# A gated attention block with eight experts on one core: new queue orders and cheaper gated sums in the last stage

## The chip, the cores and the metric

The kernel runs on one core of a Trainium2 chip. The core has TensorE (PE: matrix products, with weight loads PEld beside them), VectorE (DVE), ScalarE (ACT), GpSimd (POOL) and SyncE (SP, which here only issues DMAs). Each engine takes its own queue in order and meets the others only at semaphores. The metric is the device time of one execution in microseconds (us); lower is better.

## The reference

There are 32 sequences of 128 positions and 128 channels, all float32. Each is normalised, attends to a context (16 heads of 8 channels), and the gated result is added to x; then comes this block, whose output is again gated and added:

```python
x1 = _layer_norm(x + attn_out, ln1_w, ln1_b)           # x: normalised input of the block
gates = softmax(x1 @ gate_w.T + gate_b)                # 8 experts
top_gates, top_idx = top_k(gates, 2)
expert_outputs = einsum('bsd,efd->bsef', x1, expert_w) + expert_b
moe_out = sum(expert_outputs[top_idx] * top_gates)
out = x + tanh(g_ffn) * _layer_norm(x1 + moe_out, ln2_w, ln2_b)
```

## The kernel before

The first part, both attentions (`pe_attention`, `dve_attention` and so on), takes some two thirds of the span and isn't touched except for its constants. It leaves every sequence's attention result in `att_all` and the block's input in `xn2_all`.

The last stage (`z_pe`, `z_act`, `z_dve`, `z_pool`, `z_sp`) works on 16 groups g of two sequences (G = 2, W = 256 columns, NE = 8 experts, HALF = 4). It is a software pipeline written out by hand: every engine runs steps s = -1 to 20, and in step s its queue holds work of several groups, s to s - 4, in a fixed order; semaphores give the data order. For one group the work goes like this:

- ScalarE copies the attention result (`fetch`, z_att), TensorE transposes it (`transpose_att`), ScalarE copies that (`copy_att`, z_att_t), TensorE multiplies by the output weights (`project`).
- VectorE adds the input (`attention_sum`, z_h) and makes mean and variance; GpSimd makes the factor of the norm (`factor1`: z_ve, then a power, z_rstd); VectorE normalises (`normalise1`, z_n); GpSimd applies weight and bias (`x1`: z_nw, z_x).
- TensorE transposes z_n (`transpose_n`), ScalarE copies it with weight and bias (`copy_x1`, z_x_t). TensorE makes the logits (`logits`), then experts 0 to 3 (`experts`, k = 0, one product of 512 columns for each sequence) and, a step later, experts 4 to 7 (k = 1).
- Gates: VectorE adds the bias and takes the maximum (`shift_logits`), ScalarE takes the exponentials (`gates_exp`), VectorE finds the two best of eight and scales (`gating`: MAX8, z_sum, z_two, z_rsum, MATCH_REPLACE8, z_top, z_gates). z_two is a copy of the two largest values into a tile whose other six places hold -1.
- Experts 0 to 3 are gated and summed on VectorE in eight instructions (`experts` in `z_dve`, z_acc, on top of z_x). Experts 4 to 7 are gated on ScalarE in eight instructions (`gate_experts`, z_gated) and summed by TensorE through products with the identity (`gated_sum`), together with the experts' bias times the transposed gates (`gates_t`, `copy_gates`). For each sequence that is one product with the bias and four with the identity, 128 columns each.
- VectorE adds both halves (`all_experts`, z_x_moe) and makes the second norm's mean and variance, GpSimd its factor (`factor2`, z_rstd_), VectorE normalises (`normalise2`, z_y), GpSimd applies weight, bias and the residual (`final`: z_yw, z_ywb, z_o), SP stores (z_out).

The order on each queue in a step, with the group that each belongs to, is the `body` of each function. On VectorE it is:

```python
shift_logits(s - 2); normalise1(s - 1); normalise2(s - 4)
gating(s - 2); experts(s - 2); attention_sum(s); all_experts(s - 3)
```

Float32 products are recorded as two MATMUL entries each, so "x8" of a group is four products.

## Time and profile before

| | |
|---|---|
| median of three runs | 482.83 us (482.69 to 483.07) |
| the profiled execution | 483.01 us |
| its span, first to last instruction | 480.8 us |
| mean granted TensorE clock | 0.975 |
| busy share TensorE, VectorE, ScalarE, GpSimd | 87%, 80%, 57%, 65% |

The profile is of one execution. A row of a timeline gives the start on the span's clock, the time from the start of the first to the end of the last instruction that is merged into it (xN), and in brackets how long the engine stood idle before it and what released it. "f32<-f32" shapes are partitions x elements in each partition. A granted clock of 1.00 is 2.4 GHz for TensorE, 0.50 is 1.2 GHz. Instructions of one engine overlap by some tens of ns, so durations add up to a little more than the queue's time; where that matters, starts are compared.

### The profile page before, as it was taken

To read this page: it belongs to the slowest core of one execution; us is meant where nothing else is said; L and a number is where in the kernel's file an instruction comes from. 1 tells how busy PE (TensorE), PEld (TensorE's weight loads), DVE (VectorE), ACT (ScalarE), POOL (GpSimd) and SP (SyncE) were. 2 spreads that over 40 slices of the span, in tenths; PEclk is the share of its full clock that TensorE was granted. 3 is DMA by queue.
4 is the path that set the end of the run, shared out by engine and by line. 5 is a ranking of instruction groups with operands and counts; after the bars stand their busy time and mean duration, and the time that the engine had idled before them with its cause. 6 is when DMAs were issued, how large, how long until landed. Compare 5 with 4: busy or idle time off the path is not lost.

```text
span 480.8 us, 18054 instructions
## 1 busy us (share of the span) xinstructions
PE 420.6 (87%) x6804; PEld 265.6 (55%) x6804; DVE 382.6 (80%) x1205; ACT 273.5 (57%) x693; POOL 313.5 (65%) x688
## 2 busy tenths in 40 slices
PE   0378888888888999999999999997899999999983
PEld 0245454544445566666666666664467676767652
DVE  5688999999978878788877787832679899999971
ACT  1136777777676666675666666673354545454440
POOL 5465766767798888878887874220346666666654
PEclk9999999999999999999999999997699999999995
DMA  7855776755533444333344334200000000000000
GB/s 165 195 151 161 194 187 166 184 148 130 134 93 106 110 118 113 95 96 103 104 122 114 94 96 115 66 10 1 1 1 24 11 25 11 24 11 25 12 23 22
DMA packets 88022, 42.78 MB, mean 89 GB/s; under 512 B 15992, under 2 KB 87808, under 8 KB 87936
## 3 DMA queue, kind: packets, MB, share of 16 engines
q1 hardware_dynamic: 77072, 38.87, 30.6%
q10 hardware_dynamic: 10864, 2.76, 2.6%
q8 instruction: 55, 0.90, 0.8%
q14 instruction: 31, 0.25, 0.2%
HBM read 5.68 MB, written 2.10 MB: 16 GB/s over the span
## 4 chain that ended last, share of the span: by engine, by line
PE 37%; DVE 18%; POOL 3%; ACT 2%; issue 2%; ACTq 0%; POOLq 0%; DVEq 0%
PE u_bank L443 8%; DVE z_acc L969 5%; PE s_bank L381 5%; PE s_bank L394 4%; PE s_bank L799 2%; PE u_bank L820 2%; DVE r L617 2%; PE st_bank L799 2%; PE t_bank L373 2%; POOL z_rstd_ L697 2%; PE t_bank L367 2%; PE u_bank L456 2%; PE st_bank L394 2%; DVE z_two L945 1%; DVE z_y L994 1%
## 5 line engine op out<-in xcount | busy, mean ns | idle before, releaser
L636 DVE TENSOR_REDUCE nm<-s_bank 128x4 f32<-128x512 f32 x256 | 171.5, 682 | 37.6 <-PE s_bank L394 34.6
L526 ACT ACTIVATE pt<-st_bank 128x512 f32<-128x512 f32 x256 | 149.1, 601 | 77.2 <-PE u_bank L443 41.1
L394 PE MATMUL s_bank<-qk 64*64 64x128 bf16 (+1 forms) x1536 | 102.5, 221 | 12.2 <-DVE nm L636 7.7
L443 PE MATMUL u_bank<-pt,vaug 128*32 128x128 f32 x2048 | 109.5, 286 | 1.6 <-DVE ao L653 0.3
L394 PE MATMUL st_bank<-qk 64*64 64x128 bf16 (+1 forms) x1588 | 101.7, 218 | 0.0
L394 PEld LDWEIGHTS s_bank<-qk 64*64 64x64 bf16 (+1 forms) x1536 | 72.9, 104 | 36.1 <-issue 18.8
L394 PEld LDWEIGHTS st_bank<-qk 64*64 64x64 bf16 (+1 forms) x1588 | 72.1, 103 | 0.0
L443 PEld LDWEIGHTS u_bank<-pt,vaug 128*32 128x32 f32 x2048 | 40.8, 108 | 27.2 <-issue 3.8
L381 PE MATMUL s_bank<-mqk,idb 64*64 64x256 bf16 x256 | 38.3, 291 | 2.7 <-ACT pt L526 0.8
L884 ACT ACTIVATE z_gated<-s_bank,z_gates 128x128 f32<-128x128 f32 x64 | 18.3, 369 | 35.7 <-PE u_bank L820 35.7
L381 PE MATMUL st_bank<-mkq,idb 64*64 64x256 bf16 x256 | 38.3, 293 | 0.1
L290 POOL TENSOR_TENSOR part<-r,part 128x512 bf16<-128x512 f32 x32 | 37.1, 1159 | 1.4
L820 PE MATMUL u_bank<-z_gated,idf 128*128 128x128 f32 x256 | 38.0, 293 | 0.0
L799 PE MATMUL s_bank<-ewt,z_x_t 128*128 128x512 f32 x64 | 36.1, 647 | 0.5 <-DVE z_acc L969 0.5
L301 POOL TENSOR_SCALAR mst<-nm 128x16 bf16<-128x16 f32 x64 | 13.2, 207 | 34.3 <-DVE nm L636 34.3
L820 PEld LDWEIGHTS u_bank<-z_gated,idf 128*128 128x128 f32 x256 | 31.8, 195 | 4.0 <-issue 0.2
L799 PE MATMUL st_bank<-ewt,z_x_t 128*128 128x512 f32 x64 | 33.6, 607 | 0.0
L456 PE MATMUL u_bank<-idf,us 128*128 128x128 f32 x128 | 28.0, 300 | 5.4 <-ACT us L542 5.4
L533 ACT ACTIVATE mts<-m_bank 128x128 bf16<-128x128 bf16 x64 | 17.8, 278 | 24.5 <-PE m_bank L451 24.5
L695 POOL TENSOR_SCALAR z_ve<-z_mv 128x2 f32<-128x2 f32 x16 | 3.1, 193 | 43.7 <-DVE z_mv L913 43.6
L381 PEld LDWEIGHTS s_bank<-mqk,idb 64*64 64x64 bf16 x256 | 14.5, 103 | 26.8 <-issue 18.4
L285 POOL TENSOR_SCALAR part<-r 128x512 bf16<-128x512 f32 x32 | 19.9, 620 | 13.4 <-DVE r L617 7.1
(121 smaller groups left out, 883.0 us busy)
## 6 DMA issues: line engine op xcount, KB each, us to landing
qk<-part SPq DMA_DIRECT2D x221, 128.0 KB, 2.8
x_all<-x SPq DMA_DIRECT2D x16, 128.0 KB, 2.8
qk<-qrow SPq DMA_DIRECT2D x32, 64.0 KB, 2.2
qk<-mts ACTq DMA_DIRECT2D x64, 32.0 KB, 2.5
out<-z_o SPq DMA_DIRECT2D x16, 128.0 KB, 1.8
c_all<-ctx_in SPq DMA_DIRECT2D x14, 128.0 KB, 3.2
ewt<-exp_t SPq DMA_DIRECT2D x1, 512.0 KB
qk<-part ACTq DMA_DIRECT2D x3, 128.0 KB, 2.7
```

The source lines that it names most:

```text
L285: pool.tensor_scalar(part[u % 2][:, 1:2 * PARTS:PARTS, :], r32[:, :].rearrange("c (o t) -> c o t", o=2), 1.0, 0.0, ALU.mult, ALU.add).then ...
L290: pool.tensor_tensor(part[u % 2][:, 2:2 * PARTS:PARTS, :], r32[:, :].rearrange("c (o t) -> c o t", o=2), part[u % 2][:, 1:2 * PARTS:PARTS, ...
L381: pe.matmul(to, idb[rows, rows], mask[rows, rows].unsqueeze(1).broadcast_to([64, HEADS, 64]), start=True, stop=False, skip_group_check=True)
L394: ins = pe.matmul(to[outs, :], fixed[:, outs], moving, start=not masked, stop=True, skip_group_check=masked)
L443: ins = pe.matmul(u_bank[b][32 * j:32 * j + 32, r * P:(r + 1) * P], v, pt[m % 4][:, j, :], start=half == 0, stop=half == 1, skip_group_che ...
L456: ins = pe.transpose(u_bank[q % 2][:, W + r * P:W + (r + 1) * P], us[q % 2][:, r * P:(r + 1) * P], idf[:, :])
L526: act.activation(pt[m % 4][:, :, :].rearrange("k j q -> k (j q)"), st_bank[m % 2][:, :], ACT.Exp).then_inc(ex, 1)
L636: dve.tensor_reduce(nm[q % 2][:, first:first + HEADS], s_bank[n % 2][:, :].rearrange("q (j k) -> q j k", j=HEADS), AX_X, ALU.max, negate=T ...
L799: ins = pe.matmul(e_bank[b][k][:, :], zx1t[i][:, b * P:(b + 1) * P], ewt[:, k * 512:(k + 1) * 512], start=True, stop=True)
L820: ins = pe.matmul(dst, idf[:, :], zyg[:, b, e, :], start=False, stop=e == HALF - 1)
L884: ins = act.activation(zyg[:, b, e, :], e_bank[b][1][:, e * P:(e + 1) * P], ACT.Copy, scale=zg[i][:, b, HALF + e:HALF + e + 1])
L969: dve.scalar_tensor_tensor(out=zacc[i][e % 2][:, b, :], in0=e_bank[b][0][:, e * P:(e + 1) * P], scalar=zg[i][:, b, e:e + 1], in1=zacc[i][( ...
```

## The change

1. VectorE: `normalise2` leaves its queue. The copy z_two goes: the six smaller places of z_sorted are filled with -1 in place. `gated_pairs` is new: it adds z_gated of experts 4, 5 to those of 6, 7 for both sequences in one instruction of 512 elements in each partition (z_gated_pairs). `gating` and `gated_pairs` move ahead of `normalise1`.
2. ScalarE: `fetch` goes (TensorE transposes straight from `att_all`), `normalise2` comes as two activations (z * factor + offset), and `copy_gates` moves ahead of `copy_x1`.
3. TensorE: the gated sum takes both sequences at once: one product of 256 columns with the bias (the gates of both sequences transposed together to 16 rows, the bias laid out twice on the diagonal in `ebs`), and two of 256 columns with the identity. The order in a step becomes experts 1, transpose_att, gated_sum, gates_t, transpose_n, project, logits, experts 0.
4. GpSimd: `factor2` also makes the offset -mean * factor (one element for each sequence). `x1` now comes first in a step, `final` after it and a step later; the store is a step later too.
5. Constants: one more DMA (25 instead of 24) brings the second copy of the bias; `ebs` (16 x 256) is set to zero at the start, and SP waits for that.

```diff
-                elif 9 <= s <= 10:
-                    later_constants(sp, 3 * s - 9, 3 * s - 6)
+                elif 9 <= s <= 10:
+                    later_constants(sp, 4 * s - 18, min(4 * s - 14, LATER))
...
+                pe.transpose(u_bank[1][0:G * NE, W:W + P], zg[i][:, :, :].rearrange("q b e -> q (b e)"), idf[:, :]).then_inc(z_gt, 1)
+
+            def gated_sum(g, gc):
+                i = gc % 2
+                pe.wait_ge(z_gtc, g + 1)
+                pe.wait_ge(z_yp, g + 1)
                 if gc >= 1:
                     pe.wait_ge(z_all, (g - 1) * ALL + 1)
-                for b in range(G):
-                    ins = pe.transpose(u_bank[0][0:NE, W + b * P:W + (b + 1) * P], zg[i][:, b, :], idf[:, :])
-                ins.then_inc(z_gt, 1)
-
-            def gated_sum(g, gc):
-                i = gc % 2
-                pe.wait_ge(z_gtc, g + 1)
-                pe.wait_ge(z_yg, g + 1)
-                for b in range(G):
-                    dst = u_bank[0][:, b * P:(b + 1) * P]
-                    pe.matmul(dst, zgt[i][:, b * P:(b + 1) * P], ebs[:, :], start=True, stop=False)
-                    for e in range(HALF):
-                        ins = pe.matmul(dst, idf[:, :], zyg[:, b, e, :], start=False, stop=e == HALF - 1)
+                dst = u_bank[0][:, 0:W]
+                pe.matmul(dst, zgt[i][:, :], ebs[:, :], start=True, stop=False)
+                for e in range(HALF // 2):
+                    ins = pe.matmul(dst.rearrange("q (b d) -> q b d", b=G), idf[:, :], zyp[:, :, e, :],
+                                    start=False, stop=e == HALF // 2 - 1)
                 ins.then_inc(z_yb, 1)

             def body(s, c):
-                if in_z(c, 0):
-                    transpose_att(s, c)
                 if in_z(c, 2):
                     experts(s - 2, c - 2, 1)
                 if in_z(c, 0):
-                    project(s, c)
+                    transpose_att(s, c)
+                if in_z(c, 3):
+                    gated_sum(s - 3, c - 3)
+                if in_z(c, 2):
+                    gates_t(s - 2, c - 2)
                 if in_z(c, 1):
                     transpose_n(s - 1, c - 1)
-                if in_z(c, 3):
-                    gated_sum(s - 3, c - 3)
+                if in_z(c, 0):
+                    project(s, c)
                 if in_z(c, 1):
                     logits(s - 1, c - 1)
                     experts(s - 1, c - 1, 0)
-                if in_z(c, 2):
-                    gates_t(s - 2, c - 2)
...
+            def normalise2(g, gc):
+                act.wait_ge(z_rs2, (g + 1) * 4)
+                if gc >= 2:
+                    act.wait_ge(z_fin, (g - 2) * FIN + 1)
+                for b in range(G):
+                    act.activation(zy[gc % 2][:, b, :], zsum[:, b, :], ACT.Identity, bias=znb2[:, b:b + 1],
+                                   scale=zrs2[:, b:b + 1]).then_inc(z_y2s, 1)
...
+                if in_z(c, 4):
+                    normalise2(s - 4, c - 4)
+                if in_z(c, 2):
+                    copy_gates(s - 2, c - 2)
                 if in_z(c, 1):
                     copy_x1(s - 1, c - 1)
-                if in_z(c, -1):
-                    fetch(s + 1, c + 1)
                 if in_z(c, 2):
                     gate_experts(s - 2, c - 2)
-                    copy_gates(s - 2, c - 2)
...
-                dve.tensor_copy(ztwo[:, :, 0:2], z8[:, :, 0:2]).then_inc(z_gate, 1)
+                dve.memset(z8[:, :, 2:NE], -1.0).then_inc(z_gate, 1)
...
+            def gated_pairs(g, gc):
+                dve.wait_ge(z_yg, g + 1)
+                if gc >= 1:
+                    dve.wait_ge(z_yb, g)
+                dve.tensor_tensor(zyp[:, :, :, :], zyg[:, :, 0:HALF // 2, :], zyg[:, :, HALF // 2:HALF, :],
+                                  ALU.add).then_inc(z_yp, 1)
...
-                    dve.tensor_scalar(zy[:, b, :], zsum[:, b, :], zmv2[:, b, 0:1], zrs2[:, b:b + 1],
-                                      ALU.subtract, ALU.mult).then_inc(z_y2s, 1)
...
                 if in_z(c, 2):
                     shift_logits(s - 2, c - 2)
+                if in_z(c, 3):
+                    gated_pairs(s - 3, c - 3)
+                if in_z(c, 2):
+                    gating(s - 2, c - 2)
                 if in_z(c, 1):
                     normalise1(s - 1, c - 1)
-                if in_z(c, 4):
-                    normalise2(s - 4, c - 4)
                 if in_z(c, 2):
-                    gating(s - 2, c - 2)
                     experts(s - 2, c - 2)
...
+                rstd_of(pool, zmv2[:, :, 1], zve2[:, :], zrs2[:, :], z_rs2, g * 4)
+                pool.wait_ge(z_rs2, g * 4 + 2)
+                for b in range(G):
+                    pool.tensor_scalar(znb2[:, b:b + 1], zmv2[:, b, 0:1], zrs2[:, b:b + 1], -1.0,
+                                       ALU.mult, ALU.mult).then_inc(z_rs2, 1)
...
-                if in_z(c, 4):
-                    final(s - 4, c - 4)
                 if in_z(c, 1):
                     x1(s - 1, c - 1)
+                if in_z(c, 5):
+                    final(s - 5, c - 5)
...
+            sp.wait_ge(c_two, 1)
...
-            dve.memset(ztwo[:, :, :], -1.0).then_inc(c_two, 1)
+            dve.memset(ebs[:, :], 0.0).then_inc(c_two, 1)
```

## Rows read from the trace of the kernel before

**Rows 1.** Stretches: busy us (instructions) of each engine, granted clock, DMA share, GB/s.

```profile
20.00:40.00 20.00, 15.17 (x164) 8.79 (x164) 15.60 (x33) 6.96 (x16) 10.02 (x27) 1.00 0.59 159
331.00:334.00 3.00, 2.31 (x8) 1.53 (x8) 0.30 (x1) 0.76 (x3) 0.00 (x0) 0.50 0.00 0
414.20:422.30 8.10, 8.10 (x44) 5.53 (x43) 7.42 (x36) 4.17 (x16) 5.44 (x9) 1.00 0.07 19
```

**Rows 2.** Timeline, VectorE, one step: start us, us, engine, line, instruction.

```profile
414.21 0.60 DVE L994 TENSOR_SCALAR z_y<-z_x_moe,z_mv_,z_rstd_ 128x128 f32<-128x128 f32 x2 [0.33 <-POOL z_rstd_ L697]
414.73 0.23 DVE L942 MAX8 z_sorted<-z_exps 128x8 f32<-128x8 f32 x2
...
415.00 0.65 DVE L945 COPY z_two<-z_sorted 128x4 f32<-128x4 f32 x1
...
416.75 0.35 DVE L969 SCALAR_TENSOR_TENSOR z_acc<-s_bank,z_gates,z_x 128x128 f32<-128x128 f32 x1
...
421.07 0.14 DVE L930 TENSOR_TENSOR z_logit<-u_bank,gbb 128x16 f32<-128x16 f32 x1
...
421.37 0.60 DVE L922 TENSOR_SCALAR z_n<-z_h,z_mv,z_rstd 128x128 f32<-128x128 f32 x2
422.29 0.60 DVE L994 TENSOR_SCALAR z_y<-z_x_moe,z_mv_,z_rstd_ 128x128 f32<-128x128 f32 x2 [0.33 <-POOL z_rstd_ L697]
```

**Rows 3.** All instructions of one tile, duration ns min/median/max: z_two, then z_top.

```profile
L945 DVE COPY z_two<-z_sorted x16: 169/648/651, 340.4 to 463.0; 128x4 f32<-128x4 f32 x16
...
L952 DVE TENSOR_TENSOR z_top<-z_exps,z_others x16: 175/376/381, 341.3 to 463.7; 128x16 f32<-128x16 f32 x16
```

**Rows 4.** Timeline of GpSimd over the same step.

```profile
414.90 0.73 POOL L1029 TENSOR_TENSOR z_yw<-z_y,l2w 128x256 f32<-128x256 f32 x1 [0.72 <-DVE z_y L994]
...
418.02 0.73 POOL L1022 TENSOR_TENSOR z_x<-z_nw,l1b 128x256 f32<-128x256 f32 x1
420.13 0.19 POOL L695 TENSOR_SCALAR z_ve<-z_mv 128x2 f32<-128x2 f32 x1 [1.39 <-DVE z_mv L913]
420.41 0.70 POOL L697 TENSOR_TENSOR z_rstd<-z_ve,mhalf 128x2 f32<-128x2 f32 x1
```

**Rows 5.** Timeline of VectorE at the kernel's start.

```profile
1.25 0.07 DVE L1123 MEMSET z_two<- 128x16 f32 x1
```

**Rows 6.** Timeline of VectorE at 8.7 us.

```profile
8.73 0.69 DVE L612 TENSOR_TENSOR r<-t_bank,part 128x512 f32<-128x512 f32 x1
```

**Rows 7.** Timeline of TensorE over the same step.

```profile
416.18 0.48 PE L818 MATMUL u_bank<-ebs,z_gates_t 8*128 8x128 f32 x2
...
419.09 0.51 PE L787 MATMUL u_bank<-gwt,z_x_t 128*128 128x8 f32 x4
...
420.39 1.02 PE L799 MATMUL st_bank<-ewt,z_x_t 128*128 128x512 f32 x2
421.25 0.38 PE L809 MATMUL u_bank<-idf,z_gates 128*8 128x128 f32 x2
```

**Rows 8.** Timeline of ScalarE: one step's exponentials, and the last gated experts.

```profile
421.95 0.47 ACT L866 ACTIVATE z_exps<-z_logit,z_max 128x8 f32<-128x8 f32 x2
...
466.72 1.14 ACT L884 ACTIVATE z_gated<-s_bank,z_gates 128x128 f32<-128x128 f32 x4 [4.05 <-PE u_bank L820]
```

**Rows 9.** Timeline of VectorE: the first z_acc of three steps.

```profile
351.82 0.35 DVE L969 SCALAR_TENSOR_TENSOR z_acc<-s_bank,z_gates,z_x 128x128 f32<-128x128 f32 x1
...
457.47 0.35 DVE L969 SCALAR_TENSOR_TENSOR z_acc<-s_bank,z_gates,z_x 128x128 f32<-128x128 f32 x1
...
464.40 0.35 DVE L969 SCALAR_TENSOR_TENSOR z_acc<-s_bank,z_gates,z_x 128x128 f32<-128x128 f32 x1
```

**Rows 10.** Timeline of TensorE at the stage's start.

```profile
331.21 0.66 PE L761 MATMUL t_bank<-idf,z_att 128*128 128x128 f32 x2 [1.21 <-ACT z_att L846]
```

**Rows 11.** Timeline of VectorE, then of GpSimd, in the last steps.

```profile
473.27 0.42 DVE L980 TENSOR_TENSOR z_x_moe<-u_bank,z_acc 128x256 f32<-128x256 f32 x1 [3.70 <-PE u_bank L820]
...
476.28 0.72 POOL L1029 TENSOR_TENSOR z_yw<-z_y,l2w 128x256 f32<-128x256 f32 x1 [0.71 <-DVE z_y L994]
```

More of the change, by code:

```diff
@@ L43 @@
 AHEAD = 4
-LATER = 24
+LATER = 25
 LATE_STEP = 12
@@ L700, in two @@
             return [sb(f"{name}{i}", shape) for i in range(2)]
-        zat = two("z_att", [P, G, P])
         zo_t = two("z_att_t", [P, W])
@@ L721, in gated_block_kernel @@
         z_gate = sem("z_gate_steps"); z_exp = sem("z_gate_exp"); z_gt = sem("z_gates_transposed")
-        z_gtc = sem("z_gates_t_copied"); z_y = [sem(f"z_experts{k}") for k in range(2)]; z_yg = sem("z_experts_gated"); z_yb = sem("z_expert_bias")
+        z_gtc = sem("z_gates_t_copied"); z_y = [sem(f"z_experts{k}") for k in range(2)]; z_yg = sem("z_experts_gated"); z_yp = sem("z_gated_pairs_summed"); z_yb = sem("z_expert_bias")
         z_acc = sem("z_accumulated"); z_all = sem("z_all_summed_steps"); z_rs2 = sem("z_rstd2_steps"); z_y2s = sem("z_normalised2")
@@ L731, in z_steps @@
         def z_steps(body):
-            for s in range(-1, GROUPS + 5):
+            for s in range(GROUPS + 6):
                 body(s, s)
@@ L760, in transpose_att @@
                 for b in range(G):
-                    ins = pe.transpose(t_bank[:, b * P:(b + 1) * P], zat[i][:, b, :], idf[:, :])
+                    ins = pe.transpose(t_bank[:, b * P:(b + 1) * P], one(att_all, g * G + b), idf[:, :])
                 ins.then_inc(z_ot, 1)
```

60 lines of the change are left out of this document (26 added, 34 removed).

## The prediction

> **What bounds the kernel now.** I read the profile in this order: the page, the stretches, then the timeline of each engine over one step of the last stage, then the stage's first and last steps. The edit touches only that stage, which runs from the last attention product at about 331 us to the end of the span at 480.8. The stretches show what kind of stage it is: over one step TensorE is busy 8.10 of 8.10 us and VectorE 7.42, ScalarE 4.17, GpSimd 5.44, at full granted clock [rows 1]. So two engines are full at once. TensorE has no gap in a step, and VectorE's queue sets its length, 8.08 us: the second normalisation of one step starts at 414.21 and of the next at 422.29 [rows 2]. The chain that ended last follows VectorE through these steps. A cut that serves only one of the two would stop at once at the other; this edit cuts both.
>
> **VectorE, step by step.** Four things leave its queue or get cheaper, one comes.
>
> - The two z_y instructions go to ScalarE. They hold the queue from 414.21 to 414.73, 0.52 us, and it stood 0.33 us for their factor before; from z_n at 421.37 to z_y at 422.29 are 0.92 us where two such instructions alone need 0.52 [rows 2]. Away: 0.52 + 0.40 = 0.92.
> - The copy z_two lasts 0.17 us at its shortest and 0.65 in the median of 16 [rows 3]. In the step shown it started at 415.00, GpSimd's z_yw ran from 414.90 to 415.63, and the copy ended at 415.65 [rows 2, 4]: it was let in as GpSimd's instruction ended. In its place comes a fill of 12 elements, for which the fill of 16 elements, 0.07, is the nearest row [rows 5]. Freed: between 0.40 (if its start still costs some 0.25) and 0.58; I take 0.46.
> - z_top lasts 0.38 in the median against 0.17 at its shortest [rows 3]; I read it as the same contact. In the new order GpSimd stands waiting for z_n, which VectorE makes only after the gates, so it is idle through the gating. Freed: 0.20 (0 if something else of GpSimd falls there).
> - The sum in pairs is one VectorE instruction of 512 elements a row with both inputs in SBUF. No such row exists. The nearest is the 512-element subtraction with one input in PSUM, 0.69 us [rows 6]; the last 0.08 overlaps the next instruction, as in the pair of z_y (0.60 long, 0.52 held). I take 0.61, with 0.55 and 0.75 as ends.
>
> That is 8.08 - 0.92 - 0.46 - 0.20 + 0.61 = 7.11 us a step if nothing waits.
>
> **The wait for GpSimd.** The sum in pairs has what slowed z_top, two inputs in SBUF, so it may have to wait for GpSimd too. Let T be the end of z_n. GpSimd's five big instructions take from 414.90 to 418.75, 3.85 us [rows 4]; in the new order they follow z_n at once, so z_ve starts near T + 3.9 and the power behind it, 0.28 later and 0.70 long [rows 4], runs from 4.2 to 4.9. VectorE starts z_acc at T - 0.08, reaches the logits 4.32 later (416.75 to 421.07) and is through with them 0.30 after that (421.37) [rows 2]: the sum in pairs is due at T + 4.54, inside the power. If the power holds it off as z_yw did the copy, it gets in about 0.1 before the recorded end, at 4.81: a wait of 0.27. Ends: 0 if so small an instruction as the power doesn't hold it off, and 0.73 if it always arrives with a GpSimd instruction just begun. I take 0.27: **7.38 us a step, 0.70 less.**
>
> On this the Trainium skill (SBUF — State Buffer, section "SBUF: two separate sides") has a rule: a VectorE instruction with two SBUF inputs, or in a two-port mode, and a GpSimd instruction exclude each other for a whole instruction, whoever starts first. The rows of z_two and z_top agree. By the rule the step is 7.38 or up to 7.84; without it 7.11.
>
> **Do the others keep up?** TensorE: the gated sum takes 2.91 us now (416.18 to 419.09: ten products of 128 columns) [rows 7]. A product of 512 columns takes 0.86 (420.39 to 421.25) [rows 7], so one of 256 about 0.43 and three 1.3, with 0.1 to change over: 1.4, ends 1.3 and 1.9 (six times the 0.29 that 128 columns cost now, and the same 0.1). One of two gate transposes goes, 0.1. TensorE needs 8.1 - 1.5 - 0.1 = 6.5 us. Its order is the other danger: the second half of the experts, the gated sum and the gate transposes now stand ahead of the transposes of z_n. It restarts after z_acc, T + 2.1; experts 0 and 1 are four products of 512 columns, 3.5, the transpose of the next attention about 0.2: T + 5.8. There the pairs are ready (4.81 + 0.69 = 5.5), the gated sum ends at 7.2, the gate transpose at 7.3, and z_n of the next step is there at 7.38. Were it late, it would catch up where it now waits for z_acc: its queue alone, with about 0.4 for the copy of z_n's transpose in which it has only the projection to do, needs 6.9.
>
> ScalarE gives up the copy of the attention and gets two rows of 128 elements. By its z_gated row (four in 1.14, some 0.25 apart) [rows 8] and for two per-row operands more, 0.25 to 0.45 each; it had 4.2 of 8 us, so this hides. GpSimd gets two factors of one element a row, some 0.2 each beside a z_ve of 0.19 [rows 4]: 5.9 us with its gaps become 6.4, plus 0.6 in which the sum in pairs holds it: 7.0 of 7.38, still hidden, but with little left. The exponentials, 0.47 us for the pair [rows 8], run under the sum in pairs; were that shorter, MAX8 would wait for them, so the cover is needed.
>
> **The whole.** Between the second group's gating and the fifteenth's lie 13 steps, z_acc at 351.82 to 457.47, 105.65 us [rows 9]; at 7.38 they are 95.9, 9.7 less. The last interval, to 464.40, is 6.93 [rows 9]; new it holds z_acc 2.08, the second norm's sums 1.11 (what is left of the 4.32 beside z_acc and the first norm's 1.13), logits 0.30, pairs 0.61 + 0.27 and gating 1.36 (MAX8 at 414.73 to z_acc at 416.75 is 2.02 [rows 2], less 0.66) = 5.73: 1.2 less. Steps: -10.9.
>
> Fill: the first transposes needn't wait for a ScalarE copy (1.21 us idle before them [rows 10]), worth 0.5. Against it, the second projection now stands behind the transposes of z_n and ahead of the logits, at half clock [rows 1]: 1.2 us, half in the shade of ScalarE's copy, so 0.6. Together +0.1, ends -0.5 and +1.0.
>
> Drain, from the last z_acc X (464.40) to the end, is 16.4. Before, ScalarE's gated experts started only at 466.72, X + 2.3, behind the previous gated sum, and the last sum was ready for VectorE at 473.27, X + 8.9; final began at 476.28, 4.5 before the end [rows 8, 11]. New, they wait only for the previous pairs and the gates' transpose: X + 0.8 to 2.9, pairs to 3.7, gated sum to 5.1 (6.5 at half clock, which I take), the sums and factor 2.3 and 0.4 for the new factors: X + 9.2. But final of group 14 (three instructions of 0.73 with 0.08 between [rows 4], 2.3) now stands on GpSimd behind that factor and ahead of final of group 15: X + 9.2 + 2.3 + 4.5 = X + 16.0, that is -0.4, and -1.8 at full clock. I take -0.5.
>
> Start: a fill of 16 rows x 256 instead of 0.07 us [rows 5] stands ahead of the rows that SP waits for, +0.2 at most, taken in full. The one more constant is a single issue of some 0.5 us in a unit that has no input loads left: nothing; uncovered, 0.5.
>
> Sum: -10.9 + 0.1 - 0.5 + 0.2 = -11.1. The profiled execution took 483.01 (span 480.8 and 2.2 around it), so **471.9 us**; the median of three runs is 0.2 lower than that execution, which I leave out as within the measurement.
>
> **Rivals.**
>
> 1. *The power holds nothing off*: 7.11 a step, but MAX8 then waits 0.05 for the exponentials, 7.16: 14 x 0.22 = 3.1 us below the forecast, **468.8 us**. For it: the power handles two elements a row for 0.70 us [rows 4], so it hardly touches the memory. Against: z_top, just as small, was held off. Chance 0.13.
> 2. *The port costs a whole instruction*: GpSimd, 7.0 us full, falls behind until its big instructions, not the power, meet the pairs or the gating; 7.84 a step (7.11 + 0.73), 0.24 less than before; 14 x 0.46 = 6.4 us above the forecast, **478.3 us**. For it: z_two lost 0.48 in this way in its median step [rows 3]. Chance 0.12.
> 3. *TensorE takes over*: its queue sets the step once the gated sum takes over 1.9 us (6.9 + 0.5), and at 2.6, that is 0.86 for each product as if it had 512 columns, the step is the 8.1 of now: **482 to 484 us**. For it: ten small products take 0.29 each now, though a quarter of 0.86 is 0.21 [rows 7], so something beside the columns costs. Against: at 0.29 for each half of a 256-column product the sum is still only 1.9. Chance 0.06, no change.
> 4. *Slower: the clock.* TensorE, no longer full, is granted 1.2 GHz in mid-stage, as in 331 to 334, where it was busy 2.31 of 3 us [rows 1]. The step then goes by TensorE, 2 x 6.5 = 13.0 us: 14 x 5.6 = 79 us above the forecast, **about 551 us**. It decides if the clock falls for more than a tenth of the stage. Against: 15.17 busy of 20 us kept 2.4 GHz in 20 to 40 us [rows 1], and here it is 6.5 of 7.4. Chance 0.04. By itself: the Trainium skill (TensorE: Matmul & The Clock Gate, Part 1) says that the clock follows how busy the engine has lately been.
>
> **How the numbers follow.** The forecast has 0.65, with 470 to 475 as its own range (step 7.25 to 7.6). Range: rival 1 and the lower half of rival 2 come in, 468 to 478; out stay rivals 3 and 4 and half of 2, 0.16. A difference under 0.2%, 1 us, is no change here. Faster 0.65 + 0.13 + 0.12 = 0.90, same 0.06, slower 0.04.
>
> **What would show it.** z_acc starts 7.4 us apart; z_top at 0.17 and the fill under 0.1; the sum in pairs recorded at 0.7 plus its wait, ending behind a power; three gated products of 0.43; TensorE standing some 0.7 us before the experts; two finals in a row at the end. The prediction is wrong if the pairs stretch beyond 1.1 us, if GpSimd never stands idle, or if the granted clock falls.

## The result: 467.8 us, 3.2% less than before

| | before | changed |
|---|---|---|
| median (lowest to highest) of 4 runs | 482.95 us (482.69 to 483.79) | 467.79 us (466.28 to 468.27) |
| ratio (95% interval) | | 0.9678 (0.9655 to 0.9701) |
| the profiled execution | 483.01 us, span 480.8 | 467.32 us, span 465.5 |

The kernel is faster by 15.2 us where 11 were forecast: the time lies 4.1 us below the forecast and 0.2 below the range. Line numbers differ by a few between the two kernels; the names of tiles are the same.

I read the changed profile as I had read the other. First the stretches: a part of the kernel that the edit doesn't touch, one step of the last stage, and two stretches of its start (busy us and instructions of PE, PEld, DVE, ACT and POOL, granted clock, DMA).

```profile
20.00:40.00 20.00, 15.12 (x162) 8.84 (x164) 15.58 (x33) 6.78 (x15) 9.91 (x27) 1.00 0.60 160
400.00:407.03 7.03, 6.82 (x29) 3.96 (x28) 6.72 (x35) 4.49 (x16) 6.05 (x12) 1.00 0.06 19
335.70:341.40 5.70, 5.66 (x14) 3.62 (x15) 3.03 (x20) 1.05 (x3) 2.59 (x5) 0.50 0.00 0
341.40:345.00 3.60, 3.15 (x14) 1.61 (x12) 2.16 (x8) 0.90 (x3) 1.21 (x2) 0.98 0.00 0
```

20 to 40 us is as before [rows 1], so the difference lies in the last stage. In a step VectorE is busy 6.72 of 7.03 us and TensorE 6.82. Next the starts of z_acc: second, fifteenth and last step.

```profile
349.55 0.35 DVE L971 SCALAR_TENSOR_TENSOR z_acc<-s_bank,z_gates,z_x 128x128 f32<-128x128 f32 x1
```

```profile
441.33 0.34 DVE L971 SCALAR_TENSOR_TENSOR z_acc<-s_bank,z_gates,z_x 128x128 f32<-128x128 f32 x1
...
447.45 0.35 DVE L971 SCALAR_TENSOR_TENSOR z_acc<-s_bank,z_gates,z_x 128x128 f32<-128x128 f32 x1
```

From 349.55 to 441.33 are 91.78 us for 13 steps, 7.06 each (one of 7.38, then 7.03), where 105.65 stood [rows 9]. The chain of work that ended last, through one step, says whose 7.03 it is.

```profile
by line: PE s_bank L800 27.8%; PE st_bank L800 17.2%; PE u_bank L818 17.1%; PE u_bank L788 12.2%; ACT z_x_t L853 11.5%; PE u_bank L816 6.2%; PE t_bank L778 4.7%; PE u_bank L807 2.2%; PE t_bank L760 2.2%; issue 1.3%
...
407.94 0.57 ACT z_x_t L853
```

It no longer touches VectorE: TensorE's queue closes on itself, with one copy of ScalarE (z_x_t) inside. TensorE over the same step:

```profile
401.52 0.61 PE L788 MATMUL u_bank<-gwt,z_x_t 128*128 128x8 f32 x4 [0.21 <-ACT z_x_t L853]
401.99 1.10 PE L800 MATMUL s_bank<-ewt,z_x_t 128*128 128x512 f32 x2
...
405.50 0.38 PE L760 MATMUL t_bank<-idf,c_all 128*128 128x128 f32 x2
405.82 0.69 PE L816 MATMUL u_bank<-ebs,z_gates_t 16*128 16x256 f32 x2
406.44 1.13 PE L818 MATMUL u_bank<-z_gated_pairs,idf 128*128 128x256 f32 x4
407.41 0.27 PE L807 MATMUL u_bank<-idf,z_gates 128*16 128x128 f32 x1
407.52 0.38 PE L778 MATMUL t_bank<-idf,z_n 128*128 128x128 f32 x2
407.74 0.61 PE L770 MATMUL m_bank<-wo,z_att_t 128*128 128x128 f32 x4
408.55 0.61 PE L788 MATMUL u_bank<-gwt,z_x_t 128*128 128x8 f32 x4 [0.21 <-ACT z_x_t L853]
```

From start to start: logits 0.47, eight halves of experts 3.51, transposes of the attention 0.32, bias product 0.62, sum of the pairs 0.97, gates 0.11, z_n 0.22, projection with ScalarE's copy 0.81; together 7.03. No gap but the 0.21 after the projection, which the copy makes. And VectorE:

```profile
401.35 0.42 DVE L908 TENSOR_TENSOR z_h<-m_bank,xn_all 128x256 f32<-128x256 f32 x1
...
403.60 0.14 DVE L932 TENSOR_TENSOR z_logit<-u_bank,gbb 128x16 f32<-128x16 f32 x1
...
403.87 0.69 DVE L980 TENSOR_TENSOR z_gated_pairs<-z_gated 128x512 f32<-128x512 f32 x1
404.51 0.24 DVE L944 MAX8 z_sorted<-z_exps 128x8 f32<-128x8 f32 x2
...
404.82 0.07 DVE L947 MEMSET z_sorted<- 128x12 f32 x1
...
405.32 0.18 DVE L954 TENSOR_TENSOR z_top<-z_exps,z_others 128x16 f32<-128x16 f32 x1
405.53 0.17 DVE L956 TENSOR_TENSOR z_gates<-z_top,z_rsum 128x16 f32<-128x16 f32 x1
405.64 0.60 DVE L924 TENSOR_SCALAR z_n<-z_h,z_mv,z_rstd 128x128 f32<-128x128 f32 x2
406.17 0.34 DVE L971 SCALAR_TENSOR_TENSOR z_acc<-s_bank,z_gates,z_x 128x128 f32<-128x128 f32 x1
```

Its work takes 4.31 from z_acc to the logits (without 0.15 in which z_h waits for the projection), 0.27 to the pairs, 0.64 from there to MAX8, 1.13 from MAX8 to z_n, 0.53 for z_n: 6.88 us. What MAX8 waits for is on ScalarE:

```profile
403.99 0.49 ACT L867 ACTIVATE z_exps<-z_logit,z_max 128x8 f32<-128x8 f32 x2 [0.45 <-DVE z_max L935]
```

The exponentials end at 404.48 and MAX8 starts at 404.51. In the last step, where they had ended 0.26 us earlier, MAX8 follows the start of the pair sum at 0.61 (445.55 to 446.16). So the pair sum fills a wait that is there in any case, and 0.03 of the 6.88 is the rest of that wait. Now GpSimd at the time of the pair sum, and every instance of the pair sum (duration ns min/median/max).

```profile
403.50 0.70 POOL L698 TENSOR_TENSOR z_rstd<-z_ve,mhalf 128x2 f32<-128x2 f32 x1
404.29 0.31 POOL L696 TENSOR_SCALAR z_ve_<-z_mv_ 128x2 f32<-128x2 f32 x1
```

```profile
L980 DVE TENSOR_TENSOR z_gated_pairs<-z_gated x16: 685/685/693, 347.3 to 451.8; 128x512 f32<-128x512 f32 x16
```

The pair sum starts at 403.87 with GpSimd's power in progress (403.50 to 404.20), as foretold, and isn't held at all. It is 685 to 693 ns in all 16: 13 of them meet a power that had begun 0.35 us or more before, the other three meet z_ve_. What gives way is GpSimd's next instruction, z_ve_, which starts under the sum: 0.31 us here, 304 ns in the median of 16, 192 at its shortest.

**Where the 15.3 us of span come from.** Start of the stage (end of the last attention tile) 330.62 to 330.82: +0.2; from there to the second z_acc 21.20 to 18.73: -2.5; the 13 steps: -13.9; the last interval 6.93 to 6.12: -0.8; from the last z_acc to the end 16.4 to 18.05: +1.65.

### The profile page after: what moved, and what is told of

It is laid out like the page before. It is cut to its first block, busy times and chain, and to the rows that moved or that the text cites. A ratio compares the mean times of both kernels' runs of the same rounds, so it can differ in the third digit from the quotient of the medians.

```text
span 465.5 us, 17610 instructions
## 1 busy us (share of the span) xinstructions
PE 399.0 (86%) x6564; PEld 240.7 (52%) x6564; DVE 372.6 (80%) x1189; ACT 280.1 (60%) x709; POOL 324.2 (70%) x720
## 4 chain that ended last, share of the span: by engine, by line
PE 51%; ACT 4%; DVE 3%; POOL 1%; issue 1%; POOLq 0%; ACTq 0%; DVEq 0%
PE u_bank L445 9%; PE s_bank L800 6%; PE st_bank L800 6%; PE s_bank L383 5%; PE u_bank L818 4%; PE s_bank L396 4%; DVE r L619 2%; PE u_bank L816 2%; PE u_bank L788 2%; ACT z_x_t L853 2%; PE t_bank L375 2%; PE t_bank L369 2%; PE u_bank L458 2%; PE st_bank L396 2%; ACT part L506 1%
## 5 line engine op out<-in xcount | busy, mean ns | idle before, releaser
L800 PE MATMUL s_bank<-ewt,z_x_t 128*128 128x512 f32 x64 | 35.0, 629 | 0.0
L544 ACT ACTIVATE us<-u_bank 128x256 f32<-128x256 f32 x64 | 24.9, 389 | 0.7 <-PE u_bank L445 0.7
L646 DVE RECIPROCAL rec<-u_bank 128x16 f32<-128x16 f32 x64 | 15.9, 249 | 11.2 <-PE u_bank L458 11.2
L245 POOL TENSOR_TENSOR rstd<-ve,mhalf 128x2 f32<-128x2 f32 x32 | 22.8, 713 | 2.7
L458 PEld LDWEIGHTS u_bank<-idf,us 128*128 128x128 f32 x128 | 12.8, 140 | 19.0 <-ACT us L544 18.6
```

What stands on the lines that cost most here:

```text
L245: pool.tensor_tensor(rstd[u % 2][:, :], ve[u % 2][:, :], mhalf[:, :], ALU.pow).then_inc(rstd_s, 1)
L458: ins = pe.transpose(u_bank[q % 2][:, W + r * P:W + (r + 1) * P], us[q % 2][:, r * P:(r + 1) * P], idf[:, :])
L544: act.activation(us[q % 2][:, :], u_bank[q % 2][:, 0:W], ACT.Copy).then_inc(ucopy, 1)
L800: ins = pe.matmul(e_bank[b][k][:, :], zx1t[i][:, b * P:(b + 1) * P], ewt[:, k * 512:(k + 1) * 512], start=True, stop=True)
```

## The experiments

All stand against the changed kernel, but those named "before", and ratios are to the kernel before (483.1 to 483.4 us in these comparisons). Theory A: TensorE's queue sets 7.03 us and the power holds nothing off. Rival B: VectorE sets it, with waits for GpSimd in it. "Step" is z_acc to z_acc.

**1. no_pairs.** The sums in pairs go; TensorE adds eight experts in four products instead of four pairs in two.

```diff
-                for e in range(HALF // 2):
-                    ... zyp[:, :, e, :], start=False, stop=e == HALF // 2 - 1)
+                for e in range(HALF):
+                    ... zyg[:, :, e, :], start=False, stop=e == HALF - 1)
-                if in_z(c, 3):
-                    gated_pairs(s - 3, c - 3)
```

> The changed kernel without the sum in pairs: TensorE sums the four gated experts itself, with four identity products of 256 columns instead of two. VectorE's queue loses 0.64 us a step, TensorE's gets two products of 0.485. Theory A, TensorE's queue sets the changed kernel's step of 7.03 us: the step becomes 8.0, about 14 x 0.97 = 13.6 us more than the changed kernel, 481 us. Rival B, VectorE's queue sets the step and TensorE only trails it, as the prediction had it: the step falls to 6.4 to 7.0, 459 to 468 us.

Measured: 479.07 us, ratio 0.9941 (0.9911 to 0.9972), step 7.90.

```profile
405.13 1.99 PE L818 MATMUL u_bank<-z_gated,idf 128*128 128x256 f32 x8
406.96 0.27 PE L807 MATMUL u_bank<-idf,z_gates 128*16 128x128 f32 x1
```

```profile
403.20 0.24 DVE L944 MAX8 z_sorted<-z_exps 128x8 f32<-128x8 f32 x2 [0.56 <-ACT z_exps L867]
```

```profile
400.04 0.42 DVE L908 TENSOR_TENSOR z_h<-m_bank,xn_all 128x256 f32<-128x256 f32 x1 [0.93 <-PE m_bank L770]
```

VectorE's queue gets no shorter: from z_max to MAX8 it is 0.73 us with the pair sum and without it, since MAX8 waits for the exponentials. Then VectorE stands 0.93 us before every z_h. The step follows TensorE's sum, 1.83 from start to start instead of 0.97. A holds, with 0.86 us more and not the expected 0.97; but as VectorE was not relieved, this run could not have shown rival B's shorter step.

**2. no_bias_product.** Leaves out the experts' bias term, one product on TensorE.

```diff
-                pe.matmul(dst, zgt[i][:, :], ebs[:, :], start=True, stop=False)
-                ... start=False, ...
+                ... start=e == 0, ...
```

> The changed kernel without the product with the experts' bias (the output lacks that term), so 0.62 us less for TensorE in a step and nothing else moved. Theory A: TensorE falls to 6.4 us, VectorE's 6.88 us take over, the step goes from 7.03 to 6.9 and 14 x 0.15 = 2.1 us are saved, with the last gated sum at half clock shorter by 1.1 as well: 464.6 us. Rival B: only the end is shorter, 466.7 us. Were VectorE's own need less than 6.88, down to TensorE's 6.4: 459 us.

Measured: 464.87 us, 0.9609 (0.9580 to 0.9637), step 6.87. 0.62 us taken from TensorE shorten the step by 0.16; then VectorE is full, without an idle stretch, and TensorE waits 0.2 for z_acc. So VectorE's own need is 6.88 us, and TensorE led it by 0.15.

**3. norm2_on_vector.** z_y goes back from ScalarE to VectorE, behind z_n.

```diff
+            def normalise2(g, gc):      # VectorE
+                ...
+                    dve.tensor_scalar(zy[gc % 2][:, b, :], zsum[:, b, :], zmv2[:, b, 0:1], zrs2[:, b:b + 1],
+                                      ALU.subtract, ALU.mult).then_inc(z_y2s, 1)
                     normalise1(s - 1, c - 1)
+                if in_z(c, 4):
+                    normalise2(s - 4, c - 4)
```

> The changed kernel with the second normalisation's two instructions back on VectorE, behind the first normalisation; GpSimd's factors for it are ready by then. VectorE needs 6.88 + 0.52 = 7.4 us a step. Theory A (the larger of the two queues sets the step): 7.4 to 7.5 instead of 7.03, 14 x 0.4 = 5.6 us more, 473.4 us. If TensorE had room to spare behind VectorE (rival B) the whole 0.52 would show: 475 us.

Measured: 478.74 us, 0.9906 (0.9891 to 0.9920), step 7.79. VectorE, then GpSimd:

```profile
411.21 1.00 DVE L979 TENSOR_SCALAR z_y<-z_x_moe,z_mv_,z_rstd_ 128x128 f32<-128x128 f32 x2
```

```profile
411.38 0.75 POOL L1027 TENSOR_TENSOR z_nw<-z_n,l1w 128x256 f32<-128x256 f32 x1 [0.62 <-DVE z_n L922]
```

6.88 + 0.52 would be 7.40. The pair takes 1.00 instead of 0.60, since z_nw of GpSimd starts under it: 6.88 + 0.93 = 7.81. The move to ScalarE was worth more than its two instructions.

**4. gating_behind_norm.** VectorE makes z_n before the gates, so that GpSimd's five large instructions run beside the gating.

```diff
-                    gating(s - 2, c - 2)
-                if in_z(c, 1):
                     normalise1(s - 1, c - 1)
+                if in_z(c, 2):
+                    gating(s - 2, c - 2)
```

> The changed kernel with the gates back behind the first normalisation on VectorE. Then GpSimd's two instructions on z_n run while VectorE makes z_top and z_gates, which have two inputs in SBUF. Theory A with the exclusion by large GpSimd instructions: z_top is 0.38 long again, z_acc again waits 0.15 for the gates with nothing in between, VectorE needs 7.2 to 7.3 us a step, 470 to 472 us. If GpSimd's instructions don't hold it off: z_top stays at 0.18, step 7.03 to 7.05, 468 us.

Measured: 473.89 us, 0.9807 (0.9793 to 0.9822), step 7.45. VectorE, then GpSimd:

```profile
410.64 0.64 DVE L954 TENSOR_TENSOR z_top<-z_exps,z_others 128x16 f32<-128x16 f32 x1
```

```profile
410.52 0.73 POOL L1019 TENSOR_TENSOR z_nw<-z_n,l1w 128x256 f32<-128x256 f32 x1
```

z_top is held until z_nw ends (0.64 us, 0.176 in the changed kernel, and more than the 0.38 expected), and the first z_acc starts 0.27 after z_gates instead of 0.11. MAX8 no longer waits: 6.88 - 0.03 + 0.46 + 0.16 = 7.47, VectorE's queue. The power, which here starts under the pair sum, takes 1.05 instead of 0.70. The order of the change, with no large instruction of GpSimd beside the gating, is worth 0.4 us a step.

**5. sum_covers_copy.** On TensorE the gated sum goes between the transposes of z_n and the projection, to fill the 0.4 us of ScalarE's copy.

```diff
-                if in_z(c, 3):
-                    gated_sum(s - 3, c - 3)
                 if in_z(c, 2):
                     gates_t(s - 2, c - 2)
                 if in_z(c, 1):
                     transpose_n(s - 1, c - 1)
+                if in_z(c, 3):
+                    gated_sum(s - 3, c - 3)
```

> The changed kernel with one move on TensorE: the gates' transpose and the transposes of z_n go ahead of the gated sum, so that ScalarE's copy of the transposed z_n runs beside the gated sum and not beside the projection alone (TensorE's 0.36 us gap before the logits). Theory A: TensorE needs 6.7 us, VectorE's 6.9 take over, 14 x 0.13 = 1.8 us less than the changed kernel, 466.0 us. Rival B (VectorE sets the step already): 467.8, no change. A third way: the gated sum, 0.3 us later, makes the second sum on VectorE wait, 468 or more.

Measured: 474.30 us, 0.9819 (0.9804 to 0.9834), step 7.56. A miss. VectorE:

```profile
406.01 0.42 DVE L908 TENSOR_TENSOR z_h<-m_bank,xn_all 128x256 f32<-128x256 f32 x1 [0.59 <-PE m_bank L770]
```

TensorE's own gap is gone, but the projection is 1.6 us later, z_h waits 0.59 for it, and then TensorE waits for the gates and for z_n (0.37 and 0.24). The loop now runs through both engines and is longer than either queue.

**6. last_final_early.** On GpSimd the last step but one finishes before the last step's factors.

```diff
-                if in_z(c, 5):
+                if in_z(c, 5) and s - 5 != GROUPS - 2:
                     final(s - 5, c - 5)
+                if s - 4 == GROUPS - 2:
+                    final(s - 4, c - 4)
```

> The changed kernel with the last steps of GpSimd reordered: the final part of group 14 stands ahead of the last group's factor, not behind it. Theory: in the changed kernel two final parts stand one after the other at the end, the first of them, 2.3 us, on the path; here it fits into GpSimd's idle 2.0 us before the last factor, which it may delay by 0.3: 2.0 us less, 465.8 us. If the end isn't set by GpSimd's queue: 467.8.

Measured: 466.16 us, 0.9649 (0.9635 to 0.9664); 17.2 us from the last z_acc to the end, against 18.05.

```profile
452.86 0.67 PE L816 MATMUL u_bank<-ebs,z_gates_t 16*128 16x256 f32 x2 [3.12 <-DVE z_gated_pairs L980]
453.46 1.22 PE L818 MATMUL u_bank<-z_gated_pairs,idf 128*128 128x256 f32 x4
```

Here the last sum ran at full clock (1.82 us from start to end, 3.2 in the changed kernel), which explains 1.4 us, more than the 0.85 gained, so nothing is left for the order: the earlier finish ends at 457.70, delays the last factor (z_ve_ at 457.79, its input ready at 455.94), and the last z_yw then waits 0.99 us for ScalarE.

**7. filler_products.** Products into a bank that nobody reads, six while the stage starts and seven before the last gated sum, to keep TensorE at work.

```diff
+                if s == 1:
+                    filler(u_bank[0], 6)
+                if s == GROUPS + 2:
+                    filler(t_bank, 7)
```

> The changed kernel with products whose result nobody reads in two places where TensorE stands: six of 256 columns after the second group's first transposes (it stands 2.96 us there) and seven before the last gated sum (3.13 us). Theory: the granted clock falls to 1.2 GHz because TensorE stands, and 5.7 us of the start and the last gated sum (3.27 us) run at half speed; kept busy, the start saves 1.5 to 2.5 us and the end 1.5: 464 to 465 us. If the clock falls all the same: 467.8, or 0.5 more if the filler delays the work behind it.

Measured: 465.01 us, 0.9621 (0.9607 to 0.9636). Stretches of its start:

```profile
334.50:336.00 1.50, 1.50 (x5) 1.12 (x5) 0.31 (x3) 0.00 (x0) 0.91 (x2) 0.50 0.00 0
336.00:338.00 2.00, 2.00 (x11) 1.66 (x10) 0.43 (x2) 0.00 (x0) 1.42 (x2) 0.80 0.03 8
```

The clock falls all the same, but comes back at about 337 instead of 341.4; the fillers themselves hold up the transposes of z_n by 1.2 us. Stage start to second z_acc is 17.39 us (18.73), the last sum runs at full clock, the end takes 16.6. That the fillers keep the clock up at the end isn't shown, since the last sum begins at full clock in experiments 2 and 6 too, which have none.

**8. combined** (5, 6 and 7 together).

> The three moves together: gated sum beside ScalarE's copy, last final part early, filler products in both gaps. By the single expectations 1.8 + 2.0 + 3.5 = 7.3 us less than the changed kernel, 460.5 us; if only the first final part and the filler count, 462.3.

Measured: 472.37 us, 0.9767 (0.9751 to 0.9783), step 7.56: the order of 5 spoils the steps; 1.9 us better than 5 by itself, less than the 4.4 that 6 and 7 gained singly; both of them had the last sum at full clock already, and the clock falls at 330.9 here and comes back at 337.8, so that half clock lasts 6.8 us and not 3.4 as in 7.

**9. project_then_sum.** The gated sum goes behind the projection.

```diff
                 if in_z(c, 0):
                     project(s, c)
+                if in_z(c, 3):
+                    gated_sum(s - 3, c - 3)
                 if in_z(c, 1):
                     logits(s - 1, c - 1)
```

> The changed kernel with another order on TensorE: gates' transpose, transposes of z_n, projection, gated sum, logits. Behind z_n come the transposes and the projection at once, so VectorE's next first norm doesn't wait for a projection that stands behind the gated sum, as it did for 0.59 us a step in the run with the sum ahead of the projection, and ScalarE's copy runs beside the projection and the sum. Theory A: TensorE needs 6.7 us, VectorE's 6.88 set the step, 14 x 0.15 = 2.1 us less than the changed kernel, 465.7 us. If some other loop through the two engines is longer than 6.9, as with that order (7.56): 467.8 or more.

Measured: 467.94 us, 0.9667 (0.9642 to 0.9693), step 7.20; a miss.

```profile
401.78 0.41 PE L778 MATMUL t_bank<-idf,z_n 128*128 128x128 f32 x2 [0.46 <-ACT z_att_t L846]
```

z_n's transposes share a bank with those of the attention, and ScalarE's copy of the attention must have emptied it: the gated sum had covered that copy, and without it TensorE stands 0.46. That the time is nevertheless the changed kernel's is a coincidence: the 13 steps cost 1.6 us more and the start 0.6, but the last interval takes 0.4 less and the end 16.3 us instead of 18.05, with the last sum all but its end at full clock.

**10. final_against_pairs.** GpSimd's last three large instructions go behind the first factor, so that they meet the pair sum.

```diff
-                if in_z(c, 5):
-                    final(s - 5, c - 5)
                 if in_z(c, 0):
                     factor1(s, c)
+                if in_z(c, 5):
+                    final(s - 5, c - 5)
```

> The changed kernel with GpSimd's final part behind the first factor and not ahead of it, so that an instruction of 256 elements a row (0.73 us) and not a power of two elements runs when VectorE comes to the sum in pairs. Theory A with the exclusion: a large GpSimd instruction in progress holds the sum in pairs until it ends, so it is recorded at 0.9 to 1.4 us instead of 0.69, VectorE needs 7.1 to 7.6 us a step, 468 to 475 us. Theory that nothing on GpSimd holds this instruction: 0.69 and a step of 7.03, 468 us.

Measured: 474.49 us, 0.9810 (0.9790 to 0.9829), step 7.68. VectorE, then GpSimd:

```profile
407.20 1.01 DVE L980 TENSOR_TENSOR z_gated_pairs<-z_gated 128x512 f32<-128x512 f32 x1
...
408.94 0.70 DVE L954 TENSOR_TENSOR z_top<-z_exps,z_others 128x16 f32<-128x16 f32 x1
```

```profile
406.95 0.72 POOL L1031 TENSOR_TENSOR z_yw<-z_y,l2w 128x256 f32<-128x256 f32 x1
407.75 1.05 POOL L1034 TENSOR_TENSOR z_ywb<-z_yw,l2b 128x256 f32<-128x256 f32 x1
```

A large instruction does hold the pair sum off: it comes at 407.20 into z_yw (to 407.67) and takes 1.01, and z_ywb, starting under it, takes 1.05. In experiment and changed kernel it is the same sum; only what GpSimd is doing differs. z_top, at 408.94, meets z_o (from 408.88) and is held as well: 0.30 for the pair sum and 0.52 for z_top make 6.88 to 7.70.

**11, 12 and 15. Two parts alone on the kernel before.** before_fill_only puts the fill of 12 elements in the place of the copy z_two; before_no_bias_product leaves out the bias products; before_fill_and_no_bias does both (the last two leave out the bias term).

```diff
-                dve.tensor_copy(ztwo[:, :, 0:2], z8[:, :, 0:2]).then_inc(z_gate, 1)
+                dve.memset(z8[:, :, 2:NE], -1.0).then_inc(z_gate, 1)
...
-                    pe.matmul(dst, zgt[i][:, b * P:(b + 1) * P], ebs[:, :], start=True, stop=False)
```

> The kernel before with one edit: the six smaller places of z_sorted are filled with -1 in place instead of the copy z_two. VectorE loses some 0.5 of its 8.08 us a step, TensorE's queue keeps 8.0. Theory A (the longer queue sets the step): the step becomes 8.0, 14 x 0.08 = 1.1 us less, 481.8 us. If VectorE alone set it: 14 x 0.5 = 7 us less, 476 us.

> The kernel before without the two products with the experts' bias (its output lacks that term). TensorE loses 0.8 of its 8.0 us a step, VectorE keeps 8.08. Theory A: the step stays 8.08, only the last gated sum shortens the end, by 0.5 to 1.0: 482.2 us. If TensorE set the step: 14 x 0.8 = 11 us less, 472 us.

> The kernel before with both single cuts: the fill in place of the copy z_two (VectorE, alone worth 0.9 us of time) and no products with the experts' bias (TensorE, alone worth 1.5; the output lacks that term). Theory A, two full queues: only together do they show, the step falls to VectorE's 7.6 and the time by 14 x 0.45 to 0.5, 6.3 to 7 us, and 0.5 for the end: 476 us. If the two effects simply add: 2.4 us less, 481 us.

Measured: 482.50 us, 0.9976 (0.9965 to 0.9987), steps of 7.90 and 8.09 in turn; 481.85 us, 0.9963 (0.9946 to 0.9981), step 8.08; together 476.62 us, 0.9877 (0.9846 to 0.9908), step 7.87. TensorE in the second, then VectorE with both cuts:

```profile
419.08 1.13 PE L799 MATMUL s_bank<-ewt,z_x_t 128*128 128x512 f32 x2 [1.15 <-DVE z_acc L968]
```

```profile
389.42 0.72 DVE L953 TENSOR_TENSOR z_gates<-z_top,z_rsum 128x16 f32<-128x16 f32 x1
```

VectorE's cut alone gives 0.9 us and TensorE's 1.5 (TensorE then stands 1.15 before the products that wait for z_acc), both together 6.7. The mean of 13 steps says what of this is the two queues: 8.13 before, 8.04, 8.11, and 7.90 together. So both engines were full, but the steps give only 3.0 of the 6.6 us by which the span is shorter, and the step isn't the 7.6 that was expected. The fill took the copy out of the way of GpSimd's large instruction, and the next instruction with two inputs in SBUF met the next large one: z_gates takes 0.72 instead of 0.17 in the last run, beside z_ywb, and z_top 0.67 or z_gates 0.59 in the first. VectorE's own need fell by 0.2 us, not by 0.5. The rest lies in the time up to the second z_acc (1.0), where half clock lasts 10.2 us instead of 13.7, and in the end (2.7), where the last sum is shorter and runs at full clock. That the total came out as expected is luck.

**13. split_experts.** Experiment 9, with the transposes of the attention between the two products of the experts' second half, so that the second product covers ScalarE's copy.

```diff
-            def experts(g, gc, k):
+            def experts(g, gc, k, between=None):
                 ...
+                    if between and b == 0:
+                        between()
...
+                att = (lambda: transpose_att(s, c)) if in_z(c, 0) else None
                 if in_z(c, 2):
-                    experts(s - 2, c - 2, 1)
+                    experts(s - 2, c - 2, 1, att)
```

> The changed kernel with TensorE's order: experts 4 to 7 of the first sequence, transposes of the next attention, experts 4 to 7 of the second sequence, gates' transpose, transposes of z_n, projection, gated sum, logits, experts 0 to 3. A product of 0.86 us now stands between the attention's transposes and those of z_n, in which ScalarE makes the copy that TensorE waited 0.46 us for with the projection-then-sum order (7.20 a step). Theory A: both loops are closed, TensorE needs 6.7 us, VectorE's own 6.88 sets the step, 14 x 0.15 less than the changed kernel: 465.7 us, with 0.5 to 1 on top if the start is shorter too. If VectorE's need isn't the floor but something else holds 7.0: 467.8.

Measured: 463.80 us, 0.9592 (0.9574 to 0.9611), step 6.88, last interval 5.73.

```profile
403.75 0.38 PE L760 MATMUL t_bank<-idf,c_all 128*128 128x128 f32 x2
403.96 1.02 PE L800 MATMUL st_bank<-ewt,z_x_t 128*128 128x512 f32 x2
```

The second product now runs where TensorE had waited for the copy, and VectorE's 6.88 sets the step, as in 2, with all work done.

**14. best_of_all.** 13, with the order of 6 at the end and fillers (five at the start, seven at the end).

> The split-experts order with filler products (five at the start, seven before the last gated sum) and the last final part early. By the single runs: 2.1 for the order, 2.8 for the filler and up to 1 for the final part (its 1.6 held a gated sum at full clock, which the filler gives already): 5 to 6 us less than the changed kernel, 462 to 463 us. If the moves eat each other as in the first combination: 465 or more.

Measured: 460.94 us (460.35 to 461.72), 0.9540 (0.9525 to 0.9554), step 6.88, second z_acc at 347.49: the best version, 6.9 us below the changed kernel.

## Why the prediction was off

**Right.** Two engines were full at once: a cut on one alone moves the step by 0.02 or 0.09 us, both by 0.23 [experiments 11, 12, 15]. z_top (0.18), the fill (0.07), and the pair sum coming inside the power were as foretold. GpSimd isn't idle through the gating, as I had it, but has only small instructions there (z_rstd_ to 405.38, the offsets from 405.48), and neither z_top nor z_gates is held. GpSimd and ScalarE stayed hidden. The clock stayed up in mid-stage. The row that rival 4 rested on, 331 to 334, shows TensorE after the clock had fallen: it was at 1.2 GHz from 330.9 on, after a microsecond (330 to 331) in which the engine did nothing.

**The step that failed** is "7.38 us a step". It measured 7.03 (7.06 as a mean of 13), and the steps gave 13.9 us instead of 9.7. Three terms of it:

- *The wait for the power, 0.27.* It measured nothing, in 13 of the 13 pair sums that met a power. I had carried the contact of z_two and z_top over to it. Experiments 4 and 10 show that the contact is real where GpSimd's instruction is a large one (z_top 0.64, pair sum 1.01), and that the pair sum is open to it. That the power hardly works on the memory may be the reason, but no run shows it; what the runs show is that it doesn't hold the pair sum off once it has been in progress for some 0.2 us (experiments 2 and 13 have the shortest such lead, 0.21). The Trainium skill (SBUF — State Buffer, "SBUF: two separate sides") has the two exclude each other for a whole instruction, whoever starts first. Experiments 4 and 10 agree (0.64, 1.01 and 1.05 us); the 685 ns beside the power, which reads its input from SBUF too, do not, and the measurement decides.
- *VectorE's own 7.11* measured 6.88. All of the 0.23 lies between MAX8 and the work behind the gates, which I had at 1.36 us and which takes 1.13: z_gates to the next start is 0.11 instead of 0.26, because z_n doesn't depend on the gates and starts in their shadow (0.15), and the fill freed 0.54, not the 0.46 taken (0.08). The pair sum holds the queue 0.61, as taken, and the wait of MAX8 for the exponentials adds 0.03.
- *TensorE's 6.9.* The gated sum took 1.59, not 1.4: the sum of the pairs 0.97 for its two products, as computed (0.86 and 0.1), but the bias product 0.62, where I had counted it as one of three equal ones. With the 0.36 by which ScalarE's copy lengthens the projection (0.81 against 0.45 before), 8.1 - 1.32 - 0.1 + 0.36 = 7.04 against 7.03 measured. TensorE, which was to stand 0.7 us before the experts, stands only 0.21, before the logits. As VectorE came out at 6.88 and not at 7.38, TensorE set the step by 0.15 us [experiments 1, 2].

So rival 1's mechanism is what happened, its wait of MAX8 for the exponentials too (0.03 for its 0.05). Its time (468.8) lies near the measured one partly by luck: its 7.16 was to be VectorE's queue, which measures 6.88, and the 7.03 is TensorE's. Rival 3's mechanism came as well, without its price. I had its threshold at a gated sum of 1.9 us, which rested on the 7.38; by the measured queues it lies at 1.59 - 0.15 = 1.44, and the sum crossed it. Rival 2 needs GpSimd to fall behind; in the changed kernel it is idle 0.29 us before z_nw.

**The start of the stage: +0.1 foretold, -2.5 measured.** The sum took half clock as given and had no term for a change of it. TensorE in the kernel before, in a new window, and then TensorE's timeline in the changed one:

```profile
344.00:345.00 1.00, 1.00 (x3) 0.36 (x2) 1.00 (x5) 0.00 (x0) 0.00 (x0) 0.69 0.08 16
```

```profile
335.74 0.69 PE L778 MATMUL t_bank<-idf,z_n 128*128 128x128 f32 x2 [2.96 <-DVE z_n L924]
```

Before, half clock lasted to about 344.6 (0.69 is the mean of half and full over that microsecond), and TensorE had worked without a gap from 338.12; in the changed kernel it does so from 335.74, after 2.96 us for z_n, and is at full clock from 341.4. What stands between the two moments runs twice as fast. In all the start has half clock for 13.7 us before and for 6.8 in the changed kernel. That this is worth microseconds is shown by experiment 7 (back at 337, 1.3 us less to the second z_acc, with 1.2 lost to the fillers). How much of the 2.5 it is can be read from runs whose half-clock stretch happens to last 10.2 us: experiment 2, which does the changed kernel's work up to the second z_acc, needs 19.59 us for it (18.73 with 6.8 us at half clock), and experiments 11 and 15, which do the old work but for the fill, need 19.90 and 19.84 (21.20 with 13.7 us). With 10.2 us of half clock the two orders are thus some 0.3 us apart (the fill counts for little there: the copy in its place took 0.17 us in the second gating), and the other 2.2 us go with the clock. As the stretch differs even between kernels that do the same work up to there, this part of the gain can't be put down to the edit with certainty.

**The last interval: -1.2 foretold, -0.8 measured.** The pair sum waits for the gated experts of ScalarE there: 0.84 us from z_max to its start, 0.09 in mid-stage. Experiment 13, with another order, has the foretold 5.73, if by other parts: the pair sum, which was to be held 0.27 by the power, is held 0.14 by GpSimd's z_o.

**The end: -0.5 foretold, +1.65 measured.** The last steps of the changed kernel, all engines:

```profile
449.17 0.27 PE L807 MATMUL u_bank<-idf,z_gates 128*16 128x128 f32 x1
...
449.65 1.09 ACT L885 ACTIVATE z_gated<-s_bank,z_gates 128x128 f32<-128x128 f32 x4
...
452.57 1.19 PE L816 MATMUL u_bank<-ebs,z_gates_t 16*128 16x256 f32 x2 [3.13 <-DVE z_gated_pairs L980]
...
455.81 0.42 DVE L989 TENSOR_TENSOR z_x_moe<-u_bank,z_acc 128x256 f32<-128x256 f32 x1 [3.33 <-PE u_bank L818]
```

With X = 447.45, the last z_acc: I had the gated experts start at X + 0.8. In ScalarE's queue they stand behind the copy of the transposed gates, and TensorE's transpose stands in the new order behind the previous gated sum: 449.17, so the experts start at X + 2.2. Pairs end at X + 5.0 (foretold 3.7). The last sum, at half clock, as taken, ends at X + 8.4 (6.5): from pairs to its end 3.3 us, not 2.8. Factors are there at X + 11.25 (9.2); from there it goes on for 2.3 and 4.5 as foretold. The half clock, which the forecast had in it, costs 1.4 of the 18.05: the same two lines take 3.2 us here and 1.82 in experiment 6.

Summed up: steps -4.2, start -2.6, last interval +0.4, end +2.15 against the forecast, together -4.2. The terms for the ends were each off by 2 us or more and nearly cancelled, which is luck: the miss of the whole is as large as that of the steps. The lower end of the range, 468, was the forecast with rival 1's steps; an error of the start, or of TensorE's and VectorE's own queues, was not in it.

## What to carry to other kernels

When two engines are within a few per cent, write out both queues from start to start, with each turnaround and the copy that one of them waits for: the bound is what comes out, and an order that closes a gap on one engine can open a longer loop through both (5) or another gap (9). Put a contact between engines into the sum by what the other engine is doing at that moment, a small instruction or a large one, and put an independent instruction right behind the one whose result is awaited. Taking out the instruction that was held doesn't remove the contact: the next one with two inputs in SBUF can meet it (experiments 11 and 15). Where a stage starts or ends on TensorE at half clock, give the clock a term of its own; here it was worth 1.4 us at the end, as much as 0.1 us in every step, and some 2 us at the start.

## What the runs showed of the hardware

- The exclusion between VectorE and GpSimd isn't the same both ways. A power of two elements a row that is in progress doesn't hold the pair sum off (685 to 693 ns, 13 of 13), yet one that starts under a pair sum is held by it: 1.04 and 1.05 us instead of 0.70 [experiments 3, 4], and a z_ve_ 304 ns instead of 192. Whether a power holds a pair sum that comes less than 0.2 us after its start was not seen.
- TENSOR_SCALAR with one large SBUF input is held as well: 1.00 us for z_y's pair instead of 0.60 [experiment 3].
- A product of 16 rows into 256 columns took no less time than one of 128 rows: the bias product 0.62 us from start to start, the two products that sum the pairs 0.97, so 0.62 and 0.49 each.
- The last gated sum ran at half clock in the changed kernel after 3.13 us of standing and at full clock in experiment 6 after 3.12: the wait just before it doesn't settle it by itself. What does was not tried.
